# Scores of a graph attention layer computed a second time, transposed, in place of transposing the exponentials; a separate order of work for each engine

## The reference

```python
def euler_step(h, _):                       # first layer, 8 steps of dt = 1/8
    ax = jnp.einsum('nm,bmd->bnd', adj_mx, h)
    f = alph * 0.5 * (ax - h) + h @ w_eff - h + x0
    return (h + dt * f, None)
...
mask = jnp.where(adj == 0, -jnp.inf, 0.0)   # second layer, 4 heads of 32
scores = jnp.einsum('bhid,bhjd->bhij', q, k) / np.sqrt(HEAD_DIM) + mask
attn = jax.nn.softmax(scores, axis=-1)
out = jnp.einsum('bhij,bhjd->bhid', attn, v)
...
x = _layernorm(x + _L0_gnn_ref(x, adj, ...), axis=-1)
x = _layernorm(x + _L1_gnn_ref(x, L1_gnn_W, adj), axis=-1)
```

## Time and profile before

| | |
|---|---|
| median of 3 runs | 718.61 us (718.28 to 720.04) |
| profiled execution | 720.18 us |
| its span on the core | 718.3 us |
| PE busy | 674.5 us, 94% |
| DVE busy | 445.3 us, 62% |
| ACT busy | 407.6 us, 57% |
| POOL busy | 71.6 us, 10% |

### The profile page before, as it was taken

How to read it: one execution, slowest core, us unless ns; L and a number is a source line. 1 busy time by engine, 2 the same in 40 slices (tenths; PEclk the granted TensorE clock), 3 DMA queues, 4 the chain that set the end, 5 groups by cost and what they waited for, 6 DMA issues and landing times.

```text
span 718.3 us, 12334 instructions
## 1 busy us (share of the span) xinstructions
PE 674.5 (94%) x3793; PEld 508.9 (71%) x3793; DVE 445.3 (62%) x1280; ACT 407.6 (57%) x903; POOL 71.6 (10%) x85
## 2 busy tenths in 40 slices
PE   5997789999999999999999999999999999997783
PEld 3766667777777777878687777787877878675541
DVE  5343126567575857576666767675857576666774
ACT  3121226666665766666666666665766666657561
POOL 5000010001010001001010101010000101000001
PEclk9998999999999999999999999999999999998798
DMA  3000012211303040303121121303040312121120
GB/s 106 1 0 16 0 41 63 63 41 38 82 23 97 1 113 4 95 22 80 37 65 52 50 67 33 84 19 98 0 108 8 91 27 74 31 63 41 45 58 30
DMA packets 37183, 35.35 MB, mean 49 GB/s; under 512 B 7584, under 2 KB 24352, under 8 KB 37152
## 3 DMA queue, kind: packets, MB, share of 16 engines
q1 hardware_dynamic: 37152, 34.96, 18.8%
HBM read 5.57 MB, written 4.19 MB: 14 GB/s over the span
## 4 chain that ended last, share of the span: by engine, by line
PE 86%; DVE 6%; issue 3%; ACT 2%; DMA 1%; POOL 0%; SPq 0%; POOLq 0%; DVEq 0%; ACTq 0%
PE psE L693 13%; PE psL L596 9%; PE psL L598 8%; PE psL L597 8%; PE psO L704 8%; PE psS L607 8%; PE psL L588 5%; PE psL L590 5%; PE psL L589 5%; PE psM L667 4%; PE psL L658 3%; PE psM L672 2%; PE psS L538 2%; DVE Yl L807 2%; PE psL L583 2%
## 5 line engine op out<-in xcount | busy, mean ns | idle before, releaser
L445 ACT ACTIVATE E<-Sm,negmax 128x512 f32<-128x512 f32 x256 | 183.9, 719 | 116.1 <-DVE negmax L838 115.8
L838 DVE CUSTOM_DVE_ANT_0 Sm<-psS,mask 128x512 f32<-128x512 f32 x256 | 171.9, 686 | 91.9 <-PE psS L607 83.6
L693 PE MATMUL psE<-ident,E 128*128 128x128 f32 x960 | 143.3, 275 | 3.3 <-ACT E L445 3.3
L693 PEld LDWEIGHTS psE<-ident,E 128*128 128x128 f32 x960 | 116.3, 141 | 40.6 <-issue 19.6
L607 PE MATMUL psS<-Ks,Qs 96*128 96x512 f32 x256 | 116.9, 477 | 6.2 <-DVE negmax L838 3.4
L493 ACT ACTIVATE ET<-psE 128x512 f32<-128x512 f32 x120 | 70.6, 589 | 42.2 <-PE psE L693 42.2
L871 DVE COPY ET<-psE 128x512 f32<-128x512 f32 x120 | 82.3, 686 | 17.9 <-PE psE L693 17.9
L382 POOL TENSOR_TENSOR rstd<-var,minus_half 128x4 f32<-128x4 f32 x32 | 32.3, 1009 | 529.2 <-DVE var L821 529.2
L807 DVE TENSOR_TENSOR z<-psL,z 128x512 fp32r<-128x512 f32 x48 | 33.0, 691 | 57.8 <-ACT z L438 57.8
L607 PEld LDWEIGHTS psS<-Ks,Qs 96*128 96x128 f32 x256 | 48.0, 193 | 22.3 <-DVE negmax L838 16.1
L704 PE MATMUL psO<-ET,V 128*32 128x512 f32 x512 | 59.9, 608 | 1.9 <-issue 1.7
(11 more groups left out here) (137 smaller groups left out, 970.9 us busy)
## 6 DMA issues: line engine op xcount, KB each, us to landing
Qs<-qh SPq DMA_DIRECT2D x128, 64.0 KB, 2.0
Ks<-kh SPq DMA_DIRECT2D x128, 64.0 KB, 2.0
xin<-in_x_dram SPq DMA_DIRECT2D x16, 256.0 KB, 2.9
Qs<-ql SPq DMA_DIRECT2D x64, 64.0 KB, 2.0
Ks<-kl SPq DMA_DIRECT2D x64, 64.0 KB, 2.0
out_dram<-y SPq DMA_DIRECT2D x16, 256.0 KB, 2.3
E<-in_adj_dram SPq DMA_DIRECT2D x4, 256.0 KB, 3.6
W_sb<-in_L_gnn_W_dram SPq DMA_DIRECT2D x1, 192.0 KB, 3.4
```

Of the source, the lines that this page charges most:

```text
L445: nc.scalar.activation(E[:, h % 2, i, :], Sm[:, i % 2, :], ACT.Exp, scale=-1.0, bias=negmax[:, h * NT + i:h * NT + i + 1], accum_out=sums[ ...
L693: last = nc.tensor.transpose(e_bank(horner, i)[:, t * P:(t + 1) * P], E[:, n % 2, t, i * P:(i + 1) * P], ident[:, :])
L838: V_.tensor_tensor_reduce(out=Sm[:, i % 2, :], in0=psS[i % 2][:, :], in1=mask[:, i, :], scale=-SCALE, scalar=3e38, op0=ALU.add, op1=ALU.mi ...
```

## The change

- The transposes TR and their copies go, and so does E. ACT's exponential of a block (S) writes over Sm, and only its sum is used further.
- New are the transposed scores ST: PE multiplies the same stacked operands the other way round, Ks as the stationary side and Qs as the moving one, into one of two banks psT. DVE adds the transposed mask `maskT` and writes ET, and ACT takes the exponential in place. There are 16 such blocks for each graph. They belong to END, one iteration later than the transposes did.
- The row's maximum now lies along the columns, so it goes into the product: Qs gets two rows more (the high and low part of the negated maxima, scaled), Ks two rows of ones, 98 rows in all for ST; S uses the first 96 as before. Once all blocks of a graph are through `maximum`, PE transposes negmax into psM (MT), ACT writes the high part Mh, DVE the low part Ml, and SP sends both into the row of Qs with two DMAs. V on PE waits for MT's low part, because both use psM.
- Qs, Ks and negmax have two buffers, one for even and one for odd graphs. A stack waits for the ST of the graph that held the buffer, and its first DMA for KL, where before the Qs part waited for QL only.
- The one table of events becomes one for each engine, ten in all. CB, the sums' reciprocal (REC), XS and the layer norms change places in them; XS stands in the first third of ACT's order rather than past the middle.
- SP's order is now: load, stacks of heads 0 and 1, the maxima, stack of head 2, store, stack of head 3.
- Pool takes over the residual add and the four scalings of layer norm 2.
- The setup gets 16 transposes of the adjacency matrix on PE and four mask passes on DVE, and Pool writes the ones.

On PE at the end of an iteration of the loop (V and the scores S0), before: psE<-ident,E is a TR block, psS<-Ks,Qs a block of scores.

The diff, cut to its core:

```diff
+PE_EVENTS = [
+    ("ST", 0, 0), ("ST", 0, 1), ("S", 1, 0), ("S", 1, 1), ("Z", 1, 0), ("S", 1, 2), ("ST", 0, 2), ("UT", 0, 0),
...
+SP_EVENTS = [
+    ("STK", 0, 0), ("STK", 1, 0), ("MT", 0, 0), ("STK", 2, 0), ("LN2B", 0, 0), ("STK", 3, 0),
...
-        Qs = sb("Qs", [P, H, N], F32R)
-        Ks = sb("Ks", [P, H, N], F32R)
+        Qs = sb("Qs", [P, 2, H, N], F32R)
+        Ks = sb("Ks", [P, 2, H, N], F32R)
...
@@ SP @@
+                    if kind == "MT":
+                        sp.wait_ge(mt_lo, a + 1)
+                        for row, part in enumerate((Mh, Ml)):
+                            sp.dma_start(f(Qs[KS + row:KS + row + 1, j, :, :]), f(part[:, :])).then_inc(mt_in, 16)
+                    elif kind == "STK":
+                        if end:
+                            sp.wait_ge(st_mm, s_unit(e, n, NT))
+                        if n == 0:
+                            sp.wait_ge(m_ev, MPB * p + 3)
+                        stack(Qs, (qh, ql, qh), n)
+                        stack(Ks, (kh, kh, kl), n)
+                    elif kind == "LN2B":
+                        store()
@@ Pool @@
+            nc.gpsimd.memset(f(Ks[KS:KT, :, :, :]), 1.0).then_inc(ones_in, 1)
...
+                    elif kind == "LN2A":
+                        pool.wait_ge(c_ev, e + 1 + C_FREE)
+                        nc.gpsimd.tensor_tensor(att[:, :, :], att[:, :, :], x1res[:, j, :, :],
+                                                ALU.add).then_inc(z_done, 1)
...
+                        inverse_root(1, e)
+                        pool.wait_ge(root[1], e + 1)
+                        pool.wait_ge(y_out, 16 * e + Y_FREE)
...
+                            ins = nc.gpsimd.tensor_scalar(y[:, t, :], att[:, t, :], mv[:, 1, t, 0:1],
+                                                          rstd[:, 1, t:t + 1], ALU.subtract, ALU.mult)
+                        ins.then_inc(y_done, 1)
@@ ACT @@
-                nc.scalar.activation(E[:, h % 2, i, :], Sm[:, i % 2, :], ACT.Exp, scale=-1.0,
+                nc.scalar.activation(Sm[:, i % 2, :], Sm[:, i % 2, :], ACT.Exp, scale=-1.0,
...
-                        nc.scalar.activation(ET[:, n, i, :], e_bank(horner, i)[:, :], ACT.Copy).then_inc(t_ev[0], 1)
+                    elif kind == "MT":
...
+                        nc.scalar.activation(Mh[:, :], psM[0:H * NT, 0:P], ACT.Copy, scale=1 / SCALE).then_inc(mt_hi, 1)
+                    elif kind == "ST":
+                        act.wait_ge(st_add, s_unit(e, n, i) + 1)
+                        nc.scalar.activation(ET[:, n, i, :], ET[:, n, i, :], ACT.Exp, scale=SCALE).then_inc(st_exp, 1)
@@ PE @@
+            for m in range(NT):
+                for t in range(NT):
+                    last = nc.tensor.transpose(P_BANKS[m][:, t * P:(t + 1) * P],
+                                               adj_sb[:, t, m * P:(m + 1) * P], ident[:, :])
+                last.then_inc(a_mm, 1)
...
+            def transposed_scores(e, par, h, t):
+                s = s_unit(e, h, t)
+                if h == 0 and t == 0:
+                    pe.wait_ge(mt_in, 32 * (e + 1))
+                if t >= 2 or not isinstance(s, int) or s >= 2:
+                    pe.wait_ge(st_add, s - 1)
+                mm(psT[t % 2][:, :], Ks[0:KT, par, h, t * P:(t + 1) * P], Qs[0:KT, par, h, :],
+                   start=True, stop=True).then_inc(st_mm, 1)
...
-                        for t in range(NT):
-                            last = nc.tensor.transpose(e_bank(horner, i)[:, t * P:(t + 1) * P],
-                                                       E[:, n % 2, t, i * P:(i + 1) * P], ident[:, :])
-                        last.then_inc(t_mm, 1)
+                    elif kind == "MT":
...
+                        nc.tensor.transpose(psM[0:H * NT, 0:P], negmax[:, 1 - j, :], ident[:, :]).then_inc(mt_mm, 1)
...
+                            pe.wait_ge(st_exp, s_unit(e, H, 0))
@@ DVE @@
+            for m in range(NT):
+                dve.wait_ge(a_mm, m + 1)
+                V_.tensor_scalar(maskT[:, m, :], P_BANKS[m][:, :], 0.0, NEG, ALU.is_equal, ALU.mult).then_inc(c_vec, 1)
...
-                    elif kind == "TR" and i % 2 == 1:
-                        dve.wait_ge(t_mm, s_unit(a, n, i) + 1)
-                        V_.tensor_copy(ET[:, n, i, :], e_bank(horner, i)[:, :]).then_inc(t_ev[1], 1)
+                    elif kind == "MT":
...
+                    elif kind == "ST":
...
+                        V_.tensor_tensor(ET[:, n, i, :], psT[i % 2][:, :], maskT[:, i, :], ALU.add).then_inc(st_add, 1)
...
-                        V_.tensor_tensor(att[:, :, :], att[:, :, :], x1res[:, j, :, :], ALU.add).then_inc(z_done, 1)
...
-                    elif kind == "LN2B":
-                        dve.wait_ge(y_out, 16 * e + Y_FREE)
-                        normalise(1, e, lambda t: att[:, t, :], lambda t: y[:, t, :]).then_inc(y_done, 1)
```

More of the change, by code:

```diff
@@ L29 @@
 KS = 3 * HD
+KT = KS + 2
 PREP, ATT, END = 1, 2, 3
@@ L204, in gnn_kernel @@
         R_BANKS = [psL[0], psL[1], psO]
-        P_BANKS = psS + psE
+        P_BANKS = psS + psT
         in_w = sem("in_w")
@@ L249, in gnn_kernel @@
         m_ev = sem("m_ev")
-        stacked = [sem(f"stacked{h}") for h in range(H)]
+        stacked = [[sem(f"stacked{par}_{h}") for h in range(H)] for par in range(2)]
         s_mm = sem("s_mm")
@@ L451, in iteration @@
                 a, p, e = it - ATT, it - PREP, it - END
-                for kind, n, i in events(j, horner, prep, attend, end):
+                for kind, n, i in events(ACT_EVENTS, LATE_ACT_EVENTS, j, horner, prep, attend, end):
                     if kind == "XS":
@@ L612, in iteration @@
                 a, p, e = it - ATT, it - PREP, it - END
-                for kind, n, i in events(j, horner, prep, attend, end):
+                for kind, n, i in events(PE_EVENTS, LATE_PE_EVENTS, j, horner, prep, attend, end):
                     if kind in ("X1T", "Q", "K", "V"):
@@ L844, in iteration @@
                 a, p, e = it - ATT, it - PREP, it - END
-                for kind, n, i in events(j, horner, prep, attend, end):
+                for kind, n, i in events(DVE_EVENTS, LATE_DVE_EVENTS, j, horner, prep, attend, end):
                     if (kind, n) in L0_SPLIT:
```

209 lines of the change are left out of this document (112 added, 97 removed), and 57 rows, old and new, of tables (ACT_EVENTS, DVE_EVENTS, EVENTS, LATE_ACT_EVENTS).

## The result

The changed kernel takes **733.99 us** (median of 4 runs, 730.07 to 738.22) against 718.44 before (718.14 to 720.04). The ratio is **1.021, with a 95% interval of 1.015 to 1.028**: it is slower, where I had forecast 698 and a range of 683 to 716. Its profiled execution took 730.07 us with a span of 728.3; before, the span was 718.3. So 10.0 us of span have to be explained, and then why the other runs are up to 8 us longer still.

A forecast was written before the change was run, and what follows sets the result against it. The prediction took TensorE to bound the middle, and chains between engines the drain. Setup +2.4, filling -4.5, middle -27.7 and drain +9 summed to -20.8 us, 699.4 profiled, so a median of 698 us, range 683 to 716.

The forecast's parts named there:

- setup: Before the iterations: 16 more transposes on PE and four mask passes on DVE at 0.60 us, +2.4 us.
- iteration 2: Filling: loses 7.0 us of transposes, gets no new matmuls, held back by a chain; -4.5 us, bounds -7.0 and -3.
- the middle with iteration 15, thirteen iterations: Iterations 3 to 15: transposed scores replace transposes on PE, -2.1 us an iteration, -27.7 us in all.
- an iteration of the middle: PE's blocks 34.7 us plus 1.6 of waits from walking the four orders: 36.3, say 36.4, against 38.53 before.
- ACT's exponential of ST: ACT, 16 an iteration without accumulator: taken as 0.55 us, between a copy's 0.48 and 0.71 with accumulator.
- a scaling on Pool: Layer norm 2, 128 columns: taken as 0.3 us, between a quarter of a copy (0.15) and the root (1.01).
- drain: Last iterations: +14 us for the last one's transposed scores, -5 for iterations 16 and 17; +9, bounds +5 and +14.
- Rival (c): Middle: the loop through Pool and SP bounds, scalings at 1.0 us, an iteration 39.0; 732 us, chance 0.12.
- the SP chain from K to S0: Head 0's stacking DMAs: 7.6 us against 7.4 of PE work, just hidden at 0 to 0.3, no slack.
- rival (d): PE: the 98-row matmul isn't single-pass or costs 0.32 us; iteration about 37.0, 706 us, inside the forecast's range, no own chance.
- Rival (a): Middle: PE's floor is met, DVE and ACT hide all, an iteration 35.4 us; 685 us, chance 0.18.
- Rival (b): Middle: two-bank rings psS and psT hold PE, waits 3 us not 1.6, iteration 37.8; 715 us, chance 0.11.

The follow-up runs named there:

- the clean one: Changed kernel with the loop written out and the next x loaded ahead of the store and head 3's stack: 714.92 us, ratio 0.995.
- the two cures of the ring of two banks: Changed kernel with matmuls nothing reads in iterations 17 and 18: 731.4 us; changed kernel with four banks for transposed scores there: 731.29 us.
- the one tail: Written-out kernel with early x, plus iterations 17 and 18 merged by blocks, four banks, scalings there on DVE, root ahead of Pool's scalings: 706.74 us, ratio 0.984.
- the stack first: Kernel of 706.74 us with head 3's stack issued ahead of the store in iteration 16: 700.21 us, ratio 0.974.
- the fillers: Kernel of 700.21 us with matmuls that nothing reads added in iteration 16: 698.61 us, ratio 0.973.
- the new order: Changed kernel with last scores and maxima's transpose ahead of PV in iteration 17, layer norm 2's moments behind four mask adds: 735.47 us, ratio 1.024.

## Why the prediction was wrong, point by point

| step | predicted | measured |
|---|---|---|
| setup | +2.4 | PE's first product of iteration 0 at 59.28 (56.99 in the earlier trace rows): +2.3; its transpose of x only +1.4 |
| iteration 2 | -4.5 (-7.0 to -3) | 31.5 in place of 38.3: -6.8 |
| the middle with iteration 15, thirteen iterations | -27.7 | 481.7 in place of 493.4: -11.7 |
| an iteration of the middle | 36.4 | 36.2 to 37.3 without a turn, 39.3 to 39.6 with one; 36.24 once turn and wait for x are out |
| work of DVE and ACT in an iteration | 29.6 and 30.2 (ACT 29.0 to 32.7) | 29.2 and 28.5 in the clean one |
| ACT's exponential of ST | 0.55 | 0.51 to 0.52 |
| PE's transposed block, full clock | 0.23 | 0.23 to 0.24 |
| a scaling on Pool | 0.3 (0.15 to 1.01) | 0.78 |
| drain | +9 (+5 to +14) | +27.5 |

**The first step that failed has no term in the sum: the turn of the loop.** The walk went through one iteration and multiplied. It was right to 0.2 us (36.24 in every iteration, once the turns and the wait for x are out). But four of the iterations have a turn in them, 3 us each on DVE, and more by the clock behind it. Before, DVE's slack covered the turn, and I read the mean of 38.53 as if turns were free. This is DVE's first row of an iteration in the kernel before, in one without a turn ahead of it and in one with:

```profile
227.71 0.69 DVE L807 TENSOR_TENSOR z<-psL,z 128x512 fp32r<-128x512 f32 x1 [2.00 <-ACT z L438]
...
266.35 0.69 DVE L807 TENSOR_TENSOR z<-psL,z 128x512 fp32r<-128x512 f32 x1 [2.14 <-ACT z L438]
```

DVE waited 2 us for ACT there anyway. The row also says that the turn took DVE no more than 2.14 us before; why it takes 2.9 and more in the changed kernel no run shows.

The slack was what the change spent: DVE goes from 27.4 to 33.2 us in 40, and its last step in a round had become a wait for Pool and the moments, so the turn lies straight behind it and in front of the scores that PE wants first. Together turn, clock and the load of x are the 19 us between 733.99 and 714.92.

ACT's price:

```profile
677.88 2.17 ACT L569 ACTIVATE ET<-ET 128x512 f32<-128x512 f32 x4
```

Four exponentials in 2.17, with 0.63 for the last: (2.17 - 0.63) / 3 = 0.51.

**Rival (c) was right in its mechanism, wrong in its size, and I had mispriced its condition.** It said that the four scalings, the store, head 3's stack and the load of x form a loop that binds from 0.8 us a scaling on. They took 0.78. Its 732 us is close to what came out, but isn't made of what came out: the loop added some 0.5 us to most iterations (36.8 against 36.24) and 1.4 and 1.9 to two, not 2.6 to each, and the turn and the drain made up the rest. I took 0.3 because a root of 4 columns (1.01) seemed unlike and a copy of 512 (0.61) like it. A scaling of 128 columns with two operands per partition costs more than that copy, with a quarter of its columns. With bounds of 0.15 and 1.01 on a term that by my own sum decided the sign, 0.12 for the dear end was too sure. The Trainium skill (GPSIMD Engine Reference, Engine selection), which I had set aside as within the range, puts one input "roughly line-rate"; the row says 0.78 for 128 columns here, 0.28 on DVE (1.11 for four in the earlier trace rows).

**The drain's term failed in its structure.** I had summed what each engine has to do (28 and 17 us of DVE for two iterations) plus a chain for the last one. The trace shows 36.8 and 29.1 us for these two, 65.9 where I had counted 51. In iterations 17 and 18 each stage begins only when the one before has ended: all transposed scores, PV, division, residual, moments, and then the next graph's, because of one ET. The bundle that undoes this (8.2 us) and head 3's stack ahead of the store (6.5) gave back 14.7 of the 18.5 that I had missed; the two cures of the ring of two banks were worth 3 each, and they overlap with it (the one tail has four banks). Iteration 16 is another matter: from division to division it takes 37.9 us in the changed kernel, 38.0 with x early, 40.0 with one tail and 38.8 with the stack first. No edit shortened it, the fillers neither, and why it needs 9 us more than DVE's 29 stays open. The last iteration took 31.1 in place of 27.4: the pace was 0.79 for 0.60 (3 us), PV 5.61 for 3.64 (2), the end from the division on 10.9 for 8.15 + 1.5 (1.2), less some 2 that I had put ahead of it for the maxima, which were in time.

**What held:** PE's prices, the four orders walked, the SP chain from K to S0 (no wait of PE for head 0's stack in the steady state), the setup, and that matmuls of 98 rows cost what those of 96 do (rival (d) falls). Rival (a) falls, since even the clean iteration is 36.24 and not 35.4. Rival (b) falls: the clean iteration is 1.5 over the 34.7 without waits, and not 3. How much of the 1.5 the rings cost no run separates.

The idea itself is worth about what I forecast, in another kernel: with the loop written out, x loaded early, the drain as one stage and head 3's stack ahead of the store, it runs in 700.21 us, 2.6% below the kernel before (interval 2.3 to 2.8), and in 698.61 with fillers. That this lies by the 698 is in part luck: it has edits that the forecast didn't have, and iteration 2 gave 2.3 us more than its term.

## What to carry to other kernels

Count the turns of a loop as operations with a price and a place. Look which engine's wait hides them now, and ask whether the change spends that wait. A constant length of all iterations doesn't show that a turn is free. Of a drain, write down the chain with each buffer that makes one stage wait for the end of another, not the sum of work per engine: taking a wait out of the middle of such a stage gave at most 1 us, the order by blocks, with four banks and less on Pool, 8. And a load whose issue stands behind a wait in a queue is part of the loop that this wait closes, whatever it is needed for.

## What the runs showed of the hardware that I had not expected

- **A turn of the loop held DVE for about 3 us** (2.92 to 3.19 at the four turns of the profiled run, 3.27 to 3.79 with x loaded early), with its operands ready. Written out, these rows are gone. In the kernel before, DVE's wait at a turn was 2.14 us in place of 2.00, and an iteration with a turn only 0.1 to 0.2 longer. The Trainium skill (Advanced Engine Details and Errata, Control Flow Timing) gives a branch about 51 ns and a compare-and-branch about 108. By that, four turns would come to less than 0.5 us (an estimate from the page's figure); DVE's wait at one turn is 27 times the 108 ns or more, and the trace decides. What the engine does in that time no run shows.
- **A pause of 1.9 to 2.4 us on TensorE at such a turn was followed by a lower granted clock** (0.66 to 0.83 of full speed in a stretch of 10 us, so a part of it at the level of 1.2 GHz), and the iteration behind it lasted 1 to 2 us more. With the pauses of 1.5 to 1.9 us of the other kernels with a loop it was followed by one at 12 of 24 turns. Eight matmuls in the pause kept the clock at 1.00 in the profiled run. It is a part of why one kernel's runs scatter over 8 us where those of the written-out ones stay within 2 to 4.
- **A per-partition scaling of 128 columns took 0.78 us on GpSimd**, more than its copy of 512 columns (0.61), and was still better there than on DVE (714.92 against 720.02), which was busy for 29.2 of the 36.2 us of an iteration without the scalings.
- **PV of 32 matmuls took 3.64 us at a granted clock of 1.00, and 5.34, 5.03 and 5.61 at a mean of 0.68, 0.72 and 0.64** (the drains with fillers, with the new order, and of the changed kernel): 3.64 divided by the clock gives 5.35, 5.06 and 5.69. So a price of TensorE's work needs the clock of the place where it is used. The row of 3.64 stands in a drain as well, but in a stretch at full clock.
